# Products that nobody reads, in the pauses of TensorE at the end of attention and at the start of the experts

## The chip, the cores and the metric

The kernel runs on one core of one Trainium2 chip. The time is the device time of one execution in microseconds; of several executions the median is given. One more execution, under the hardware profiler, left the trace that the rows below come from.

## What is computed

Two stages follow each other. The first is cross attention with a causal mask, the second a routed feed-forward layer in which each token goes to one of 32 small experts.

```python
# x, ctx: (32, 256, 256) float32; 16 heads of 64; 32 experts with a hidden width of 64
q, k, v = layernorm(x) @ Wq, ctx @ Wk, ctx @ Wv            # 256 -> 1024, split into 16 heads
attn = softmax(where(causal_or_masked, -max, q @ k.T / 8))
x = x + (attn @ v) @ Wo + bo
n = layernorm(x).reshape(-1, 256)                          # 8192 tokens
e = argmax(n @ router_w.T + router_b)
x = x + relu(relu(n @ w1[e] + b1[e]) @ w2[e] + b2[e])
```

## The kernel before

**Attention phase.** Batches 0 to 31 run one after the other, and each batch in four quads of four heads (`QUADS`, index `s`). TensorE's work of a quad is written by hand in `iteration(b, prev, nxt)` (L675 ff.): the scores of the next quad in two halves, `scores(*ahead, 0, ...)` and `scores(*ahead, 1, ...)` (L584), between them the transposes of the normalised probabilities of this quad, `probs_t` (L629), then `values` of the quad before (L650, probabilities by V), then the `pieces`: projections for the next batch (L514), Wo of the batch before (L546), the transposes of its second layernorm (`x2`, L505) and its router logits (`lg`, L556). In the last batch there is no next batch, so most pieces are missing: in quad 2 only the transposes and the logits of batch 30 are left, in quad 3 none. `first_ready` and `second_ready` hold the waits ahead of `probs_t`: the probabilities must have been normalised by VectorE (L1109, L1112), which waits in turn for ScalarE's exponentials (L799).

`ranks` (L568) counts the tokens of a batch for each expert. VectorE turns these counts into row numbers (L992 to L1052), and GpSimd scatters the rows of the batch into the experts' lists in memory (L463, two scatters a batch).

**Behind the last batch** TensorE runs, in this order: ranks of batch 30, Wo of batch 31 in three parts with the last `values` between them, `busy(12)`, the transposes of batch 31 (they wait for its layernorm), `busy(2)`, its logits, `busy(6)`, ranks of batch 31 (they wait for the one-hot rows, L982), `busy(12)`. `busy(n)` issues n products of 512 columns (L673) whose results nobody reads.

**Expert phase.** The lists are cut in tiles of 128 tokens, taken in 48 pairs, u = 0, 1, 2 and so on in groups of `U` = 16. SyncE loads a pair's rows (`XS`, L1340). VectorE normalises them (`XH`, L1363) and at the end adds the residual (`Y`, L1373). TensorE does `turn` (4 transposes, L1473), `hid` (8 records, L1486) and `y_of` (4 records, L1496). ScalarE copies the transposes out (L1429) and applies relu (`HT`, L1436). GpSimd scatters the two tiles of the pair to the output (L1329). TensorE issues turn of pair u+4, hid of pair u+2 and y of pair u together; the first pairs are written out by hand (L1503 ff.), behind six unread products of 512 columns (L1503). In `hid` an unread product of 256 columns (L1483) stands ahead of each pair from u = 8 on.

A float32 product that isn't a transpose leaves two matmul records in the trace, so the six products of L1503 are 12 records; the products of `busy` leave one each.

Of the kernel before, what the change touches and what calls it, by code (L numbers as in the profile page):

```python
# [29 lines left out]
def attention_moe(nc, x, ctx, mask, Wq, Wk, Wv, Wo, bo, router_w, router_b, w1, b1, w2, b2, out):  # L30
# [21 lines left out]
    with ExitStack() as es:  # L52
# [240 lines left out]
        def G(b, s):  # L293

            return QUADS * b + s + 1
# [205 lines left out]
        def _(pe):  # L501
# [72 lines left out]
                last = transposes(dst, xn)  # L574
                last.then_inc(s_xt_pe, 1)

            def scores(b, s, i, between=None):
                p = 2 * s + i
                for it, o in ((0, 0), (1, P)):
                    if it and between:  # L580
                        between()
                    for side in range(2):
                        rows = slice(DH * side, DH * side + DH)
                        last = nc.tensor.matmul(psS[:, 2 * i + side, o:o + (it + 1) * P], QT[rows, p, it * P:(it + 1) * P],  # L584
                                                KT[rows, p, 0:(it + 1) * P], start=True, stop=True)
                last.then_inc(s_sc, 1)
# [17 lines left out]
            def first_ready(b, s, prev, nxt):  # L604

                pe.wait_ge(s_pn, 4 * G(b, s) - 2)
                if s > 0 or prev:
                    pe.wait_ge(s_pt, 3 * G(b, s) - 3)
                for bank, (name, at) in last_in(b, s, prev, nxt).items():
                    if bank < 2:  # L610
                        pe.wait_ge(*emptied(name, at))
# [57 lines left out]

            def busy(count):  # L670

                for _ in range(count):
                    nc.tensor.matmul(psS[:, 2, :], Wh["q"][:, 0, 0:P], Wh["q"][:, 0, 0:512], start=True, stop=True)  # L673

            def iteration(b, prev, nxt):  # L675
                for s in range(QUADS):
                    ahead = later(b, s + 1, nxt)
                    if ahead:
                        if s == 0 and prev and not (isinstance(b, int) and b == 1):

                            pe.wait_ge(s_pf, b - 1)
                        scores_may_start(*ahead)
                        scores(*ahead, 0, lambda: first_ready(b, s, prev, nxt))
                        probs_t(b, s, 0)
                        scores(*ahead, 1, lambda: second_ready(b, s, prev, nxt))
                        probs_t(b, s, 1)
                    else:
                        first_ready(b, s, prev, nxt)
                        probs_t(b, s, 0)
                        second_ready(b, s, prev, nxt)  # L690
                        probs_t(b, s, 1)
                    if s > 0:
                        values(b, s - 1, not prev and s == 1)
                    elif prev:
                        values(b - 1, QUADS - 1)
                    now = pieces(s, prev, nxt)
                    for n, (name, off) in enumerate(now):
                        if n < 3:
                            pe.wait_ge(s_pt, 3 * G(b, s) - 2 + n)
                        else:  # L700
                            pe.wait_ge(*emptied(now[n - 3][0], b + now[n - 3][1]))
                        piece(name, b + off, psR[:, banks(len(now))[n], :])
                        if s == QUADS - 1 and prev and n == 0:
                            ranks(b - 1, 8 * G(*ahead))
# [32 lines left out]
            values(B - 1, QUADS - 1)  # L737
            wo(B - 1, psR[:, 0, :], range(4, 6))
            wo(B - 1, psR[:, 0, :], range(6, PAIRS))
            busy(12)  # L740
            pe.wait_ge(s_xn2, 2 * B)
            transposes(psR[:, 1, :], xn2).then_inc(s_x2t_pe, 1)
            busy(2)
# [575 lines left out]
        with nc.Block(no_gpsimd_drain=True) as block2:  # L1319
# [140 lines left out]
            def _(pe):  # L1460
# [15 lines left out]
                def hid(i, u, free=True):  # L1476
                    pe.wait_ge(s_xht, U * i + u + 1)
                    for t in range(2):
                        pe.wait_ge(s_w1[t], U * i + u + 1)
                    if free:  # L1480
                        pe.wait_ge(s_h, U * i + u - 3)
                    if not isinstance(i, int) or i > 0 or u >= 8:
                        nc.tensor.matmul(psH[u % 2][:, 2 * P:4 * P], ident[:], W1R[:, 0:2, 0:P], start=True, stop=True)  # L1483
                    for c in range(KD):
                        for t in range(2):
                            last = nc.tensor.matmul(psH[u % 2][half(t), slot(u)], W1[u % W][:, t, c * HID:(c + 1) * HID], XHT[u % W][:, t, c, :],  # L1486
                                                    start=(c == 0), stop=(c == KD - 1))
                    last.then_inc(s_h_pe, 1)
# [10 lines left out]
                    last.then_inc(s_y_pe, 1)  # L1499

                pe.wait_ge(s_w1r, 16)
                for _ in range(6):
                    nc.tensor.matmul(psH[0][:, :], ident[:], W1R[:, 0:4, 0:P], start=True, stop=True)  # L1503
                pe.wait_ge(s_w2r, 32)
                pe.wait_ge(s_ht1, 1)
                turn(0, 0, False)
                turn(0, 1, False)
                hid(0, 0, False)
                turn(0, 2)
                for u in range(2):  # L1510
                    y_of(0, u, False)
# [45 lines left out]
```

## Time and profile before

| | us |
|---|---|
| median of 3 executions without the profiler | 1508.87 |
| lowest and highest of them | 1504.34, 1510.36 |
| the profiled execution, device time | 1513.0 |
| its span in the trace | 1511.3 |
| attention phase, to the last ranks | 0 to 1359.7 |
| expert phase, from the first turn | 1371.7 to 1511.3 |

The profiled execution lies above all three others. Sums are made in the trace, whose span lies 1.7 us below its device time. Granted clock 1.00 is TensorE at its full 2.4 GHz, 0.50 is 1.2 GHz. A row of the timeline gives the start of a group of like instructions, the time from its first start to its last end, and in square brackets how long the engine sat idle ahead of it and what ended that.

### The profile page before, as it was taken

How to read it: one execution, taken by the hardware profiler on the slowest of the kernel's cores; microseconds unless marked ns; L12 is line 12 of the kernel's file. 1: busy time of each engine (PE TensorE's matmuls, PEld its weight loads, DVE VectorE, ACT ScalarE, POOL GpSimd, SP SyncE). 2: the span in 40 equal slices, each digit the busy share in tenths (PEclk: the TensorE clock that was granted, in tenths of full speed). 3: DMA queues.
4: the chain of work that ended last, by engine and by line, in shares of the span. 5: the costliest groups of instructions: out<-in, count | busy, mean ns of one | idle time of the engine just before them, and what ended most of it. 6: DMA issues, size and time to landing. Idle time of an engine off the chain costs nothing.

```text
span 1511.3 us, 43956 instructions
## 1 busy us (share of the span) xinstructions
PE 1479.1 (98%) x14165; PEld 1283.4 (85%) x14165; DVE 1231.7 (82%) x5088; ACT 1013.6 (67%) x3144; POOL 360.6 (24%) x507
## 2 busy tenths in 40 slices
PE   8999999999999999999999999999999999978997
PEld 7898888888888888888888888888888888865775
DVE  5888888988888888888988888888888988755663
ACT  5767667667677667677666677677677677633663
POOL 3112212211121122222211121122222211112777
PEclk9999999999999999999999999999999999987998
DMA  8643000000000000000000000010000000005650
GB/s 288 128 150 115 29 21 29 29 22 29 29 22 25 25 29 29 27 23 29 29 22 29 28 23 22 29 29 29 23 27 29 29 22 22 15 8 175 212 174 12
DMA packets 70410, 77.85 MB, mean 52 GB/s; under 512 B 11351, under 2 KB 64221, under 8 KB 70369
## 3 DMA queue, kind: packets, MB, share of 16 engines
q1 hardware_dynamic: 62546, 60.37, 13.8%
q0 software_dynamic: 7680, 16.93, 3.1%
q8 instruction: 22, 0.36, 0.1%
q14 instruction: 18, 0.15, 0.0%
q10 hardware_dynamic: 144, 0.03, 0.0%
HBM read 47.61 MB, written 33.88 MB: 54 GB/s over the span
## 4 chain that ended last, share of the span: by engine, by line
PE 93%; DVE 3%; ACT 1%; DMA 1%; POOL 1%; issue 1%; SPq 0%; POOLq 0%; DVEq 0%
PE psR L514 37%; PE psS L584 14%; PE psO L650 12%; PE psR L546 12%; PE psR L629 6%; PE psS L1496 4%; PE psR L505 2%; PE psR L1486 2%; PE psR L556 2%; PE psR L1483 1%; PE psR L1473 1%; PE psO L1473 1%; DVE Sm L1112 0%; ACT Sm L799 0%; DMA lists<-stg,lrow 0%
## 5 line engine op out<-in xcount | busy, mean ns | idle before, releaser
L799 ACT ACTIVATE Sm<-Sm,mneg 128x128 f32<-128x128 f32 (+1 forms) x1024 | 453.5, 456 | 153.6 <-DVE mneg L1097 153.6
L1097 DVE CUSTOM_DVE_ANT_0 Sm<-psS,MK 128x128 f32<-128x128 f32 (+1 forms) x1024 | 303.7, 353 | 4.4 <-PE psS L584 1.9
L792 ACT ACTIVATE PT<-psR 128x512 f32<-128x512 f32 x384 | 201.6, 598 | 134.8 <-PE psR L629 130.9
L584 PE MATMUL psS<-KT,QT 64*128 64x128 f32 (+1 forms) x2048 | 251.5, 356 | 5.0 <-DVE V L774 2.0
L799 ACT ACTIVATION_READ_ACCUMULATOR Sm<-Sm,mneg 128x1 f32 x1024 | 205.5, 201 | 0.0
L650 PE MATMUL psO<-PT,V 128*64 128x256 f32 (+1 forms) x2048 | 196.0, 334 | 0.6 <-DVE OT_lo L1117 0.3
L1112 DVE SCALAR_TENSOR_TENSOR Sm<-Sm,halve,rinv 128x512 f32<-128x512 f32 x256 | 191.4, 748 | 0.0
L584 PEld LDWEIGHTS psS<-KT,QT 64*128 64x128 f32 x2048 | 148.7, 187 | 30.4 <-issue 7.7
L650 PEld LDWEIGHTS psO<-PT,V 128*64 128x64 f32 x2048 | 127.4, 137 | 49.0 <-DVE OT_lo L1117 1.2
L629 PEld LDWEIGHTS psR<-ident,Sm 64*128 64x128 f32 x3072 | 144.5, 139 | 21.1 <-DVE Sm L1112 2.5
L1103 DVE RECIPROCAL rinv<-rsum 128x4 f32<-128x4 f32 x256 | 44.1, 172 | 135.6 <-ACT Sm L799 132.3
L629 PE MATMUL psR<-ident,Sm 64*128 64x64 f32 x3072 | 140.9, 223 | 2.2 <-DVE Sm L1112 2.2
L1109 DVE SCALAR_TENSOR_TENSOR Sm<-Sm,halve,rinv 128x256 f32<-128x256 f32 x256 | 124.1, 485 | 9.1
L756 ACT ACTIVATE KT<-psR 128x512 f32<-128x512 f32 x128 | 75.6, 591 | 55.0 <-PE psR L514 55.0
L514 PE MATMUL psR<-CT_hi,Wk_hi 128*128 128x256 f32 x512 | 108.0, 293 | 1.3 <-ACT PT L792 1.3
L1329 POOL DMA_INDIRECT out<-Y,tok x96 | 94.0, 979 | 49.4 <-issue 27.4
L514 PE MATMUL psR<-XT_hi,Wq_hi 128*128 128x256 f32 x512 | 103.5, 284 | 2.0 <-DVE XT_lo L777 1.3
L514 PE MATMUL psR<-XT_lo,Wq_hi 128*128 128x256 f32 x512 | 103.3, 283 | 0.0
L756 ACT ACTIVATE QT<-psR 128x512 f32<-128x512 f32 x128 | 76.5, 598 | 39.8 <-PE psR L514 39.7
L514 PE MATMUL psR<-CT_lo,Wk_hi 128*128 128x256 f32 x512 | 103.0, 283 | 0.0
L514 PE MATMUL psR<-XT_hi,Wq_lo 128*128 128x256 f32 x512 | 103.0, 283 | 0.0
L514 PE MATMUL psR<-CT_hi,Wk_lo 128*128 128x256 f32 x512 | 102.7, 282 | 0.0
(155 smaller groups left out, 3061.7 us busy)
## 6 DMA issues: line engine op xcount, KB each, us to landing
lists<-pad SPq DMA_DIRECT2D x8, 1560.0 KB, 10.2
XS<-lists SPq DMA_DIRECT2D x48, 260.0 KB, 2.9
x_in<-in_x SPq DMA_DIRECT2D x32, 256.0 KB, 3.0
ctx_in<-in_ctx SPq DMA_DIRECT2D x32, 256.0 KB, 2.6
xr<-in_x SPq DMA_DIRECT2D x32, 256.0 KB, 2.6
W2R<-in_L_ffn_weights SPq DMA_DIRECT2D x1, 2048.0 KB
out<-Y,tok POOLq DMA_INDIRECT x96, 2.4
W2R<-in_L_xattn_Wv SPq DMA_DIRECT2D x2, 512.0 KB, 9.3
```

What stands on the lines that cost most here:

```text
L514: last = nc.tensor.matmul(dst, a(k), z(k), start=(n == 0), stop=(n == 3 * len(ks) - 1))
L546: last = nc.tensor.matmul(dst[:, it * D:(it + 1) * D], a[:, t, rows], z[:, t, :], start=(it == 0 and a is OTh and z is Woh and t == 0), st ...
L584: last = nc.tensor.matmul(psS[:, 2 * i + side, o:o + (it + 1) * P], QT[rows, p, it * P:(it + 1) * P], KT[rows, p, 0:(it + 1) * P], start=T ...
L629: last = nc.tensor.transpose(ring[:, o:o + DH], Sm[rows, 2 * (s % 2) + i, side, src:src + P], ident[rows, rows])
L650: last = nc.tensor.matmul(psO[DH * side:DH * side + DH, i * N + t * P:(i + 1) * N], V[:, t, DH * h:DH * h + DH], blocks_of[:, blocks, :, : ...
L756: nc.scalar.activation(T[:, 2 * c:2 * c + 2, :].rearrange("p a n -> p (a n)"), src[:, :], ACT.Copy).then_inc(done, 1)
L792: nc.scalar.activation(PT[:, s % 2, 512 * k:512 * k + 512], psR[:, k, :], ACT.Copy).then_inc(s_pt, 1)
L799: nc.scalar.activation(v, v, ACT.Exp, bias=mneg[:, s % 2, k:k + 1], scale=-1.0, accum_out=rsum[:, s % 2, k:k + 1]).then_inc(s_exp, 1)
L1097: nc.vector.tensor_tensor_reduce(out=Sm[:, 2 * (s % 2) + i, side, cols], in0=psS[:, 2 * i + side, cols], in1=MK[:, cols], scale=-SCALE, sc ...
L1109: nc.vector.scalar_tensor_tensor(out=v, in0=v, scalar=halve[:, 0:1], in1=of[:, :, 0:1].broadcast_to([P, 2, P]), op0=ALU.mult, op1=ALU.mult ...
L1112: nc.vector.scalar_tensor_tensor(out=v, in0=v, scalar=halve[:, 1:2], in1=of[:, :, 1:2].broadcast_to([P, 2, N]), op0=ALU.mult, op1=ALU.mult ...
L1329: nc.gpsimd.indirect_dma_start(out_rows, bass.IndirectOffsetOnAxis(ap=tok[u][:, t:t + 1], axis=0), Y[u][:, t, :], None, bounds_check=last_ ...
```

## The change

Five places on TensorE get more products that nobody reads. No other instruction is added, taken away or moved.

- In the last batch, quad 2: three products of 128 columns (64 rows deep) between the parts of the first half of the scores, ahead of the wait for normalised probabilities, and two in the second half.
- In the last batch, quad 3: `busy(5)` ahead of the first wait and `busy(4)` ahead of the second. `busy` itself now waits first until the last scores have been read, since it writes into their bank.
- Behind the last Wo: `busy(20)` where `busy(12)` stood.
- In `hid` the product of 256 columns stands ahead of each pair from u = 1 on, not from u = 8: seven more.
- At the start of the expert phase: seven products of 512 columns where six stood, and two of 128 columns each behind the turn of pair 0 and the hid of pair 0 (`still(2)`).

```diff
-            def scores(b, s, i, between=None):
+            def scores(b, s, i, between=None, still=0):
                 p = 2 * s + i
                 for it, o in ((0, 0), (1, P)):
                     if it and between:
+                        for _ in range(still):
+                            nc.tensor.matmul(psS[:, 2 * i, 3 * P:4 * P], ident[0:DH, :], ident[0:DH, :], start=True, stop=True)
                         between()
...
             def busy(count):
 
+                pe.wait_ge(s_sm, 8 * G(B - 1, QUADS - 1))
                 for _ in range(count):
                     nc.tensor.matmul(psS[:, 2, :], Wh["q"][:, 0, 0:P], Wh["q"][:, 0, 0:512], start=True, stop=True)
...
-                        scores(*ahead, 0, lambda: first_ready(b, s, prev, nxt))
+                        scores(*ahead, 0, lambda: first_ready(b, s, prev, nxt), 3 if s == 2 and not nxt else 0)
                         probs_t(b, s, 0)
-                        scores(*ahead, 1, lambda: second_ready(b, s, prev, nxt))
+                        scores(*ahead, 1, lambda: second_ready(b, s, prev, nxt), 2 if s == 2 and not nxt else 0)
                         probs_t(b, s, 1)
                     else:
+                        busy(5)
                         first_ready(b, s, prev, nxt)
                         probs_t(b, s, 0)
+                        busy(4)
                         second_ready(b, s, prev, nxt)
...
-            busy(12)
+            busy(20)
             pe.wait_ge(s_xn2, 2 * B)
...
-                    if not isinstance(i, int) or i > 0 or u >= 8:
+                    if not isinstance(i, int) or i > 0 or u >= 1:
                         nc.tensor.matmul(psH[u % 2][:, 2 * P:4 * P], ident[:], W1R[:, 0:2, 0:P], start=True, stop=True)
...
-                for _ in range(6):
+                for _ in range(7):
                     nc.tensor.matmul(psH[0][:, :], ident[:], W1R[:, 0:4, 0:P], start=True, stop=True)
                 pe.wait_ge(s_w2r, 32)
                 pe.wait_ge(s_ht1, 1)
+                def still(count):
+                    for _ in range(count):
+                        nc.tensor.matmul(psY[3][:, 0:P], ident[:], W1R[:, 0, 0:P], start=True, stop=True)
+
                 turn(0, 0, False)
+                still(2)
                 turn(0, 1, False)
                 hid(0, 0, False)
+                still(2)
                 turn(0, 2)
```

TensorE in the last batch, quads 2 and 3, before. `Sm` are the probabilities, `xn2` and `X2T` the second layernorm of batch 30 and its transpose:

```order
L584 MATMUL psS<-KT,QT 128x128 x2
L584 MATMUL psS<-KT,QT 128x256 x2
L629 MATMUL psR<-ident,Sm 128x64 x8
L584 MATMUL psS<-KT,QT 128x128 x2
L584 MATMUL psS<-KT,QT 128x256 x2
L629 MATMUL psR<-ident,Sm 128x64 x16
```

The same place after, on through quad 3 (the four rows of `values`, L652, left out):

```order
L586 MATMUL psS<-KT,QT 128x128 x2
L582 MATMUL psS<-ident 128x128 x3
L586 MATMUL psS<-KT,QT 128x256 x2
L631 MATMUL psR<-ident,Sm 128x64 x8
L586 MATMUL psS<-KT,QT 128x128 x2
L582 MATMUL psS<-ident 128x128 x2
L586 MATMUL psS<-KT,QT 128x256 x2
L631 MATMUL psR<-ident,Sm 128x64 x16
...
L505 MATMUL psR<-ident,xn2 128x128 x4
L556 MATMUL psR<-rwT,X2T 128x32 x4
L676 MATMUL psS<-Wq_hi 128x512 x5
L631 MATMUL psR<-ident,Sm 128x64 x8
L676 MATMUL psS<-Wq_hi 128x512 x4
L631 MATMUL psR<-ident,Sm 128x64 x16
```

The new rows stand ahead of the four waits for `Sm`, and nothing else has moved.

TensorE at the start of the expert phase, before; the number behind a name is the pair's:

```order
L1503 MATMUL psR<-W1R,ident 128x512 x6
L1473 MATMUL psO<-ident,XH0 128x128 x4
L1473 MATMUL psR<-ident,XH1 128x128 x4
L1486 MATMUL psR<-XHT0,W1_0 64x128 x4
L1473 MATMUL psO<-ident,XH2 128x128 x4
```

and after, as far as the hid of pair 1:

```order
L1508 MATMUL psR<-W1R,ident 128x512 x7
L1478 MATMUL psO<-ident,XH0 128x128 x4
L1513 MATMUL psS<-W1R,ident 128x128 x2
L1478 MATMUL psR<-ident,XH1 128x128 x4
L1491 MATMUL psR<-XHT0,W1_0 64x128 x4
L1513 MATMUL psS<-W1R,ident 128x128 x2
L1478 MATMUL psO<-ident,XH2 128x128 x4
...
L1488 MATMUL psR<-W1R,ident 128x256
L1491 MATMUL psR<-XHT1,W1_1 64x128 x4
```

Each hid from pair 1 on now has an L1488 ahead of it, and the turns of pairs 1 and 2 each have two small products ahead.

## Rows read from the trace of the kernel before

**Rows 1.** The page's second part, granted clock in 40 slices.
```profile
PEclk9999999999999999999999999999999999987998
```

**Rows 2.** Windows: length, busy of PE, PEld, DVE, ACT, POOL, clock, DMA share, GB/s.
```profile
1331.00:1341.00 10.00, 6.61 (x61) 4.82 (x60) 4.83 (x22) 6.30 (x20) 0.00 (x0) 0.66 0.01 2
1352.00:1362.00 10.00, 8.39 (x33) 6.50 (x34) 4.16 (x26) 0.60 (x1) 0.72 (x1) 0.66 0.00 1
1370.00:1375.00 5.00, 2.67 (x19) 1.55 (x17) 3.19 (x12) 1.39 (x3) 0.00 (x0) 0.96 1.01 308
1390.00:1395.00 5.00, 5.00 (x34) 4.03 (x33) 3.10 (x12) 4.00 (x10) 2.25 (x3) 0.83 0.33 106
```

**Rows 3.** Timeline of TensorE, last batch: start us, us, engine, line.
```profile
1325.92 0.70 PE L584 MATMUL psS<-KT,QT 64*128 64x256 f32 x4 [0.92 <-DVE Sm L1112]
1327.79 0.70 PE L584 MATMUL psS<-KT,QT 64*128 64x256 f32 x4 [0.65 <-DVE Sm L1112]
1332.30 1.05 PE L556 MATMUL psR<-rwT,X2T 128*128 128x32 f32 x8 [0.90 <-ACT X2T L766]
1334.47 0.69 PE L629 MATMUL psR<-ident,Sm 64*128 64x64 f32 x8 [1.12 <-DVE Sm L1112]
1336.25 1.12 PE L629 MATMUL psR<-ident,Sm 64*128 64x64 f32 x16 [1.09 <-DVE Sm L1112]
1337.64 2.83 PE L650 MATMUL psO<-PT,V 128*64 128x256 f32 x16 [0.28 <-DVE OT_lo L1117]
1343.58 1.52 PE L650 MATMUL psO<-PT,V 128*64 128x256 f32 x16
```

**Rows 4.** Timeline of all engines, behind the last Wo to the expert phase.
```profile
1348.07 2.91 PE L673 MATMUL psS<-Wq_hi 128*128 128x512 f32 x12
1349.91 0.69 DVE L943 TENSOR_TENSOR stg<-psR,xr 128x512 f32<-128x512 f32 x1 [3.44 <-DMA lists<-stg,lrow]
1353.61 0.67 PE L505 MATMUL psR<-ident,xn 128*128 128x128 f32 x4 [2.63 <-DVE xn L959]
1354.96 1.92 PE L556 MATMUL psR<-rwT,X2T 128*128 128x32 f32 x8
1356.69 2.91 PE L673 MATMUL psS<-Wq_hi 128*128 128x512 f32 x6
1358.23 0.22 DVE L982 TENSOR_TENSOR OH<-iota_e,eid 128x64 bf16<-128x64 f32 x1
1359.40 0.28 PE L568 MATMUL psS<-OH,upto 128*128 128x32 bf16 x2
1365.10 5.42 PE L1503 MATMUL psR<-W1R,ident 128*128 128x512 f32 x12 [0.62 <-DVE tile_row L1358]
```

**Rows 5.** Timeline, start of the expert phase, and the last scatter.
```profile
1371.69 0.72 PE L1473 MATMUL psO<-ident,XH 128*128 128x128 f32 x4 [1.18 <-DVE XH L1363]
1373.56 0.74 PE L1473 MATMUL psR<-ident,XH 128*128 128x128 f32 x4 [1.15 <-DVE XH L1363]
1376.08 2.07 PE L1496 MATMUL psS<-W2R,HT 65*128 x4
1391.96 1.13 PE L1496 MATMUL psS<-W2R,HT 65*128 x4
...
1394.63 0.97 POOL L1329 DMA_INDIRECT out<-Y,tok  x1 [2.45 <-DVE Y L1373]
...
1508.62 0.97 POOL L1329 DMA_INDIRECT out<-Y,tok  x1 [0.30 <-issue]
```

**Rows 6.** Timeline of TensorE, one pair with its unread product, full clock.
```profile
1397.15 0.63 PE L1473 MATMUL psO<-ident,XH 128*128 128x128 f32 x4
1397.62 0.60 PE L1483 MATMUL psR<-W1R,ident 128*128 128x256 f32 x2
1398.73 1.13 PE L1496 MATMUL psS<-W2R,HT 65*128 x4
1399.70 0.51 PE L1473 MATMUL psR<-ident,XH 128*128 128x128 f32 x3
```

## The prediction

> **What bounds the kernel now.** I read the page's slices of granted clock first. They are full but for the first slices and for two near the end [rows 1]. A change of unread products can give time only where the clock is low, so the question is what stands in those stretches. Windows over the end show three, in each of which the clock fell to 0.50, that is 1.2 GHz, and came back to 2.4 GHz. A mean of 0.66 over 10 us is 6.8 us at 0.50: once between 1331 and 1341, once between 1352 and 1362. The third is long: a mean of 0.96 up to 1375 puts its start at 1374.6, one of 0.83 from 1390 on puts its end at 1391.7 [rows 2]. Then I read the timeline for what TensorE did ahead of each fall. Ahead of the first it waited for ScalarE and VectorE: pauses of 0.92 and 0.65, then 0.90 between a few small products and 1.12 [rows 3]. Ahead of the second it sat 2.63 us [rows 4]. Ahead of the third there were pauses of 1.18 and 1.15 [rows 5]. So the falls follow pauses that add up, and the change puts products into just these.
>
> Behind these stretches another engine holds the end. From the scatter at 1394.63 to the one at 1508.62 GpSimd issues 90 scatters, 113.99/89 = 1.28 us each, with no idle time but their own 0.30 of issue between them [rows 5]. A pair has two, 2.56 us; TensorE needs 1399.70 - 1397.15 = 2.55 us for a pair [rows 6]. The end is thus "start of the unbroken row of scatters + 90 x 1.28". The time is saved only by what makes that row start earlier.
>
> **Part 1, last batch.** Quad 2 gets 3 + 2 products of 128 columns, each two records. By the nearest row, 4 transposes of 128 columns in 0.47 us (from its start to that of the next line) [rows 6], a record is 0.12: 0.7 us in a pause of 0.92 and 0.47 in one of 0.65 [rows 3]. They fit. `busy(5)` starts behind the logits, at about 1333.2; one product of it is 0.24 us at full clock (12 in 2.91 us [rows 4]), so it ends at 1334.4, ahead of the transposes at 1334.47. `busy(4)`, 0.96, fits in the 1.09 ahead of 1336.25 with 0.1 to spare. The new wait inside `busy` is for scores that VectorE finished reading at about 1331; nothing queues behind it. What the clock gives: `values` of quad 2 took 2.83 us at half speed, the same work at full speed 1.52 [rows 3]. Its start, 1337.64, stays, since it waits for VectorE's OT_lo: the 0.4 us that the transposes ahead gain are not on the path. **Gain 1.3 us**; bounds 0 (the clock falls all the same) and 1.3. It carries on: ranks of batch 30 feed VectorE, the list scatter, and L943, which waits 3.44 us for that scatter's landing and not for Wo [rows 4]. Wo itself moves up by the same 1.3, so neither takes the place of the other.
>
> **Part 2, behind the last Wo.** `busy(20)` lasts 20 x 0.24 = 4.8 where 2.9 stood, in a gap of 2.9 + 2.63: about 0.75 us of pause stay (by starts, 0.22 a product, 1.2). If the clock stays up: the logits, at 1354.96 because they wait for ScalarE's copy, take 1.05 [rows 3] instead of 1.92 [rows 4], and end at 1356.0. The one-hot rows came 1358.45 - 1356.88 = 1.57 behind the logits' end, so 1357.6. `busy(6)`, 6 x 0.24 = 1.45, is through by 1357.3 and covers itself. At half clock it took 2.91 and held the ranks until 1359.40, 0.95 behind the one-hot rows [rows 4]. Ranks now at 1357.65: **gain 1.75 us**, bounds 0 and 1.75. What is next late there is VectorE's chain to the row numbers, unchanged.
>
> Behind these ranks `busy(12)` is now over at full speed, 2.9 us after them, and the products of L1503 start 5.7 us after them (1365.10 - 1359.40 [rows 4]). The pause of 2.8 us, with one small transpose in it, is as long as the 2.63 that preceded a fall. So in part of the executions the clock will fall here. I price that at nothing: the 14 records of L1503 take 14 x 0.45 = 6.3, the pause to the first turn was 1.18 and takes the seventh product's 0.9; a low stretch as long as the first two, 6.8 us [rows 2], would cost 3.4 if it lay on these products alone; they run without a pause, which the others did not, so I take half, 1.7, which pushes the first turn by about 1.4, and the next turn waits for its rows at 1373.56 anyway [rows 5]. Bounds 0 and 2 us lost.
>
> **Part 3, expert phase.** In the clock of before, if TensorE stays at 2.4 GHz: steps are turn 0.47, unread product and hid 1.11, y 2.55 - 1.58 = 0.97 [rows 6]. y of pair 0 starts at 1376.0 as before, since it waits for ScalarE's HT; hid of pair 0, still(2) and turn 2 (0.6 + 0.47 + 0.47 from 1374.25) end at 1375.8 and lie beside that wait. y of pair 0 took 2.07 [rows 5] and takes 0.97, to 1377.0. Then hid 1 and turn 3, 1.58; y of pair 1 waits 0.4 more for its HT and runs 1379.0 to 1380.0; hid 2, turn 4, hid 3, turn 5 take 3.16, y of pair 2 runs 1383.15 to 1384.1; hid 4, turns 6 and 7, hid 5 take 3.16, y of pair 3 starts at 1387.3. Before it started at 1391.96 and its scatter followed at 1394.63, 2.67 later [rows 5]. Now its scatter is due at 1389.95. GpSimd is free by then (pair 2's two scatters end at 1388.3). From there TensorE makes a pair in 2.55 and GpSimd takes 2.56, so the row stays unbroken: **gain 4.7 us**. The unread products of pairs 1 to 5 are in this sum; those of pairs 6 and 7 hide behind GpSimd. Bounds: 4.7 up, and below zero down, which is a rival.
>
> A rule to weigh: the clock came back at 1391.7 [rows 2], just ahead of y of pair 3 at 1391.96 [rows 5], so behind the hids and turns that stand between y of pair 2 and that one, and half of these are transposes. The Trainium skill, "TensorE: Matmul & The Clock Gate", Part 4, says that in a transpose the full clock isn't engaged, since it doesn't count as busy work in the same way. By that rule the opening, rich in transposes, would stay at half speed as before, and the result would be the first rival's. The trace speaks against it.
>
> **Sum.** 1.3 + 1.75 + 4.7 = 7.75, less nothing. 1513.0 - 7.8 = 1505.2 for an execution like the profiled one. The median of before is 1508.87, so against it 3.7 us, 0.25%. The runs of before spread from 1504.34 to 1510.36; by my reading the low one is an execution in which the long low stretch was missing or short, and it checks the sum: without part 3's stretch the profiled one would be at about 1508, without any at 1505. The change should above all make the slow executions like the fast one.
>
> **Rivals.** (a) The clock falls in the opening all the same. For: after the change pauses of about 0.6 us are left ahead of turns 0 and 1, with a pause's worth of waiting on HT. Against: they are half as long as before and products stand between. Then the unread products cost up to 2 x 0.53 = 1.06 each at half clock, and five of them stand ahead of pair 3: with the same 17 us low, 1513.0 - 3.05 + 5.3 = 1515.3; with a stretch as short as the first two, about 1509. Chance 0.12. (b) The same, but the clock doesn't come back. In the half state a pair takes about 2 x 2.55 = 5.1 us against GpSimd's 2.56, so each pair beyond the fourth breaks the row of scatters and adds 2.5 us: one more pair gives 1517.8, two 1520.4. It decides as soon as the low stretch outlasts that of before. This ends slower by over 0.5% (above 1516.4). Chance 0.05. (c) The products miss: one of the first two stretches stays and the opening gains, or the other way round, or the executions of before were mostly without the long stretch; nothing is to be seen, 1507.5 to 1509.5. Chance 0.09. (d) `busy(4)` or `busy(5)` outlasts its cover because the clock has fallen before it: 0.24 more for each, 2.2 us in all, less the 1.3 of `values`; about 1 us lost, in the range, no case of its own. (e) More than forecast, below 1501.3: it would need 3.8 us that no row offers, since the main loop is untouched; 0.03.
>
> **Chances.** Forecast 0.71, rivals as given. A measurement of this kernel tells about 0.5%, 7.5 us, from no change. Faster by more 0.03; within 0.91; slower by more 0.06. The range goes from 1503.0 (a little under the fastest run of before) to 1509.5, which takes in (c) and the short form of (a).
>
> **What would show it.** In the trace after: granted clock 1.00 through 1330 to 1345 and 1350 to 1358, `values` of quad 2 at 1.5 us, ranks of batch 31 about 3.05 us earlier; no idle time of the first products beyond 0.3 us; clock 1.00 from the first turn on, y of pair 3 some 7.7 us earlier, and GpSimd's row unbroken from its fourth pair. A low stretch of about 3 us around L1503 would not matter. I am wrong if the opening still shows 0.50 over many us, if TensorE and not GpSimd ends last at the scatters, or if the transposes at 1334.47 and 1336.25 have become late.

## The result, and the profile after

| us | before | changed |
|---|---|---|
| median of 16 executions each | 1509.61 | 1504.66 |
| lowest and highest | 1504.34, 1514.36 | 1501.86, 1506.27 |
| profiled execution: device time, span | 1513.0, 1511.3 | 1501.86, 1500.1 |

The ratio is 0.9968, with a 95% interval from 0.9954 to 0.9982: 4.9 us faster by the medians, clear of noise, and within the 0.5% that had been set as "no change". 1505.2 had been forecast. The spread narrows from 10 us to 4.4.

The ratios in this text are those on record. They aren't the quotients of the medians, and where a kernel's executions fall into groups the two can differ.

The profiled execution of the changed kernel is its fastest, that of before lies near its slow end, and so their spans differ by 11.2 us, more than twice what the medians do. The clock of the two pages says why. The second part of the page after, which answers [rows 1]:

```profile
PEclk9999999999999999999999999999999999999999
```

The windows after, columns as in [rows 2]: the two of 10 us that had 0.66, the edge before the long low stretch and the 15 us inside it:

```profile
1331.00:1341.00 10.00, 9.17 (x94) 7.03 (x93) 7.66 (x40) 3.58 (x10) 0.03 (x1) 1.00 0.01 2
1352.00:1362.00 10.00, 7.51 (x30) 4.18 (x29) 6.96 (x39) 0.31 (x1) 2.04 (x2) 1.00 0.08 27
1370.00:1375.00 5.00, 4.65 (x35) 3.31 (x36) 3.38 (x12) 2.42 (x7) 2.54 (x3) 1.00 1.09 359
1375.00:1390.00 15.00, 15.00 (x110) 11.49 (x112) 9.09 (x32) 10.88 (x27) 9.15 (x10) 1.00 0.64 206
```

All three low stretches are gone. So is a fourth, which has nothing to do with the change: in the first batch, where TensorE's instructions are the same in both kernels. Windows from 24 to 34 us, first of before, then of after:

```profile
24.00:34.00 10.00, 7.38 (x50) 6.11 (x51) 6.01 (x24) 3.04 (x8) 0.50 (x2) 0.66 0.98 302
```

```profile
24.00:34.00 10.00, 7.07 (x69) 6.45 (x70) 5.86 (x25) 4.47 (x14) 0.49 (x2) 1.00 0.97 305
```

0.66 over 10 us is 6.8 us at 1.2 GHz in before, none in after. It is worth 3 us: the first scores of the last batch's quad 2 stand at 1324.51 in one trace and at 1321.53 in the other, ahead of anything the change touches. These 3 us of the 11.2 aren't the change's: of the eleven traces of this case without added products in the first batch, five show full clock there, five have 6.8 us at half clock and one 3.4.

The rest by place. The timeline after; the L652 row answers that of L650 at 1337.64 in [rows 3], the next five answer [rows 4], the last four [rows 5] (L1478 turn, L1501 y):

```profile
1330.22 1.41 PE L676 MATMUL psS<-Wq_hi 128*128 128x512 f32 x5
1331.56 0.47 PE L631 MATMUL psR<-ident,Sm 64*128 64x64 f32 x8
1334.68 1.52 PE L652 MATMUL psO<-PT,V 128*64 128x256 f32 x16 [0.69 <-DVE OT_lo L1122]
...
1348.70 0.66 PE L505 MATMUL psR<-ident,xn 128*128 128x128 f32 x4 [0.19 <-DVE xn L964]
1350.05 1.08 PE L556 MATMUL psR<-rwT,X2T 128*128 128x32 f32 x8 [0.22 <-ACT X2T L771]
1350.96 1.62 PE L676 MATMUL psS<-Wq_hi 128*128 128x512 f32 x6
1352.84 0.20 PE L568 MATMUL psS<-OH,upto 128*128 128x32 bf16 x2 [0.26 <-DVE OH L987]
1358.45 6.28 PE L1508 MATMUL psR<-W1R,ident 128*128 128x512 f32 x14 [0.62 <-DVE tile_row L1363]
...
1364.90 0.71 PE L1478 MATMUL psO<-ident,XH 128*128 128x128 f32 x4 [0.18 <-DVE XH L1368]
1368.55 1.12 PE L1501 MATMUL psS<-W2R,HT 65*128 x4
...
1380.24 1.13 PE L1501 MATMUL psS<-W2R,HT 65*128 x4
```

GpSimd's first scatter of pair 3 and the last one, answering those of [rows 5], and one between them:

```profile
1382.92 0.97 POOL L1334 DMA_INDIRECT out<-Y,tok  x1 [1.86 <-DVE Y L1378]
...
1438.53 0.98 POOL L1334 DMA_INDIRECT out<-Y,tok  x1 [0.95 <-DVE Y L1378]
...
1497.48 0.97 POOL L1334 DMA_INDIRECT out<-Y,tok  x1 [0.30 <-issue]
```

| from | to | before | after | gained | forecast |
|---|---|---|---|---|---|
| start | values of quad 2 | 1337.64 | 1334.68 | 2.96 | 0 |
| values of quad 2 | ranks of batch 30 | 2.76 | 1.46 | 1.30 | 1.3 |
| these ranks | transposes of batch 31 | 13.21 | 12.56 | 0.65 | 0 |
| the transposes | ranks of batch 31 | 5.79 | 4.14 | 1.65 | 1.75 |
| these ranks | first turn | 12.29 | 12.06 | 0.23 | 0 |
| first turn | y of pair 3 | 20.27 | 15.34 | 4.93 | 4.7 |
| y of pair 3 | its scatter | 2.67 | 2.68 | 0 | 0 |
| its scatter | last scatter | 113.99 | 114.56 | -0.57 | 0 |

In these two traces each of the three gains is within 0.25 us of its forecast. Where nothing had been forecast, 0.65 and 0.23 were gained and 0.57 lost. The 0.65 is the landing of the second list scatter: from its start to that of VectorE's L943 (L948 after), which waits for it, the traces have 3.29 us before (1346.62 to 1349.91) and 2.65 after (1342.35 to 1345.00). The change doesn't touch either.

The experiments show that these terms aren't yet the reason for the difference of the medians.

### The profile page after: what moved, and what is told of

It reads as the page before. It is cut to its first block, busy times and chain, and to the rows that moved or that the text cites. A ratio compares the mean times of both kernels' runs of the same rounds, so it can differ in the third digit from the quotient of the medians.

```text
span 1500.1 us, 44058 instructions
## 1 busy us (share of the span) xinstructions
PE 1473.2 (98%) x14216; PEld 1280.3 (85%) x14216; DVE 1230.8 (82%) x5088; ACT 1012.3 (67%) x3144; POOL 360.3 (24%) x507
## 4 chain that ended last, share of the span: by engine, by line
PE 93%; DVE 3%; ACT 1%; POOL 1%; DMA 1%; issue 1%; SPq 0%; ACTq 0%; POOLq 0%; DVEq 0%
PE psR L514 37%; PE psS L586 14%; PE psO L652 12%; PE psR L546 12%; PE psR L631 6%; PE psS L1501 3%; PE psR L505 2%; PE psR L1491 2%; PE psR L556 2%; PE psR L1488 1%; PE psR L1478 1%; PE psO L1478 1%; POOL out L1334 0%; DVE Sm L1117 0%; ACT Sm L804 0%
## 5 line engine op out<-in xcount | busy, mean ns | idle before, releaser
L652 PE MATMUL psO<-PT,V 128*64 128x256 f32 (+1 forms) x2048 | 194.7, 332 | 1.1 <-DVE OT_lo L1122 0.7
L652 PEld LDWEIGHTS psO<-PT,V 128*64 128x64 f32 x2048 | 126.7, 136 | 49.1 <-DVE OT_lo L1122 4.5
L631 PEld LDWEIGHTS psR<-ident,Sm 64*128 64x128 f32 x3072 | 143.3, 138 | 19.4 <-DVE Sm L1117 0.9
L631 PE MATMUL psR<-ident,Sm 64*128 64x64 f32 x3072 | 139.7, 221 | 0.1
L392 POOL CAST first_masked<-maskrow 128x1 f32<-128x1 uint8 x32 | 5.9, 183 | 406.6 <-DMA maskrow<-in_mask_BxS_bf 406.6
```

The source lines that it names most:

```text
L631: last = nc.tensor.transpose(ring[:, o:o + DH], Sm[rows, 2 * (s % 2) + i, side, src:src + P], ident[rows, rows])
L652: last = nc.tensor.matmul(psO[DH * side:DH * side + DH, i * N + t * P:(i + 1) * N], V[:, t, DH * h:DH * h + DH], blocks_of[:, blocks, :, : ...
```

## The experiments

Three rounds of four kernels. The first round came to a chip that takes 1548.0 us for the kernel before; the other two to one like the first (1509.2 and 1509.8). Ratios are to the kernel before of the same round.

**The products of attention alone.** Edits against the changed kernel:

```diff
-                    if not isinstance(i, int) or i > 0 or u >= 1:
+                    if not isinstance(i, int) or i > 0 or u >= 8:
...
-                for _ in range(7):
+                for _ in range(6):
...
-                still(2)      # both places
```

> Only the products of the last batch and the 20 behind the last Wo; the expert phase is that of the kernel before. My theory: ranks of batch 31 come 3 us earlier against the first scores of the last batch than in the trace of before, values of quad 2 takes 1.5 us, and the whole gains 3 us: a median near 1506.5 where the changed kernel has 1504.7. The opening of the expert phase still falls to half clock in part of the executions, so they stay spread by 6 us or more. Rival, the gain of this part is lost again in the expert phase: median at the kernel before, within 1 us.

> Only the products of the last batch and the 20 behind the last Wo, again, for a chip of the first kind. Theory as before: 3 us under the kernel before in every execution, so a median near 1506, but still spread over 6 us or more, since the opening falls to half clock in part of the executions. Rival: within 1 us of the kernel before.

On the slow chip 1542.52 against 1548.0, ratio 0.9963 (0.9949 to 0.9977). On the usual one 1501.92 against 1509.75, ratio 0.9949 (0.9931 to 0.9967), six executions from 1500.74 to 1505.73. I had expected 3 us and got 7.8, and the spread came out at 5.0 where 6 or more had been expected. By the medians this half of the change is faster alone than the whole (1501.92 against 1504.66 and 1506.07). That isn't clear of noise: the intervals of the ratios overlap, and the two never ran in the same round.

**The products of the expert phase alone.** The other half: no products in quads 2 and 3, `busy(12)` behind the last Wo.

> Only the products of the expert phase; the last batch and what stands behind its last Wo are as before. My theory: the low stretches at the last batch and behind the last Wo come back and cost 3 us, the opening stays at full clock in every execution: median near 1507.5, spread under 5 us, values of quad 2 at 2.8 us, y of pair 3 about 15.5 us after the first turn as in the changed kernel. Rival, the whole gain is the opening's: median 1504.7, like the changed kernel.

> Only the products of the expert phase, again, for a chip of the first kind. Theory: the slow executions of the kernel before go (none above 1510), its fast ones stay where they are, and the median is near 1507.5, 3 us above the changed kernel. Rival: the changed kernel's median.

Slow chip: 1543.83, ratio 0.9970 (0.9959 to 0.9981). Usual one: 1509.65, ratio 0.9995 (0.9983 to 1.0008), twelve executions from 1507.60 to 1511.62. The executions above 1512 went (the kernel before has five of 16 in this round from 1512.4 to 1514.6), but so did those below 1507.6 (it has three, from 1505.88). The median doesn't move. That the low end would stay where it is was wrong, and so was that none would lie above 1510: six of the twelve do.

Its windows over the two low stretches of attention, and over the opening:

```profile
1331.00:1341.00 10.00, 6.74 (x66) 5.29 (x67) 5.64 (x25) 5.28 (x18) 0.00 (x0) 0.83 0.00 0
1350.00:1360.00 10.00, 7.12 (x27) 5.61 (x28) 3.54 (x21) 0.60 (x1) 0.94 (x2) 0.66 0.00 1
1370.00:1390.00 20.00, 18.64 (x132) 13.58 (x131) 12.16 (x42) 11.68 (x28) 6.19 (x7) 1.00 0.86 279
```

The first two are back, the third stays away. Against it the attention half, from its first turn on:

```profile
1368.00:1388.00 20.00, 18.71 (x141) 13.96 (x140) 14.39 (x48) 14.81 (x36) 9.14 (x10) 1.00 0.90 285
```

It too is at full clock in the opening, without any product added there. So in this pair of traces, both at full clock, one can read what the opening's products cost. From the first turn to y of pair 3 it takes (turn and y of the attention half, then of the opening half, whose y is L1499):

```profile
1367.72 0.63 PE L1478 MATMUL psO<-ident,XH 128*128 128x128 f32 x4
...
1381.31 1.13 PE L1501 MATMUL psS<-W2R,HT 65*128 x4
```

```profile
1371.44 0.72 PE L1476 MATMUL psO<-ident,XH 128*128 128x128 f32 x4 [0.35 <-DVE XH L1366]
...
1387.31 1.13 PE L1499 MATMUL psS<-W2R,HT 65*128 x4
```

13.59 us without the products, 15.87 with them, 20.27 in the trace of before with the long low stretch. Against a trace whose clock falls there they save 4.4 us; against one whose clock doesn't they cost 2.3. The row of scatters adds to the cost: from the scatter of pair 3 to the last it takes 114.64 us in the opening half and 113.88 in the attention half.

**The changed kernel without the seven products ahead of the hids of pairs 1 to 7** (the line `u >= 8` again, the rest stays).

> The changed kernel without the seven products of 256 columns ahead of the hids of pairs 1 to 7; the small ones and the seven of 512 columns stay. Theory: five of them stand on the path to y of pair 3, 0.53 us each, and the turns and hids keep the clock up without them. Then y of pair 3 comes 2.6 us earlier (12.8 us after the first turn), the unbroken row of scatters starts as much earlier, and the median is about 1502.5. Rival, it is these products that hold the clock: the granted clock falls to 0.5 in the opening and the median is 1508 or more, with single executions above 1512.

> The changed kernel without the seven products ahead of the hids of pairs 1 to 7, again, for a chip of the first kind. With these products the pair of runs at a cold start differed by 2.1 us (1506.53 and 1504.42). Theory: 2 us under the changed kernel, 1503 to 1504, and no low stretch of over 7 us in the opening. Rival: more executions with a long low stretch, median 1505 or more.

Slow chip: 1541.47, 0.9957 (0.9942 to 0.9972). Usual one: 1502.24, 0.9951 (0.9934 to 0.9967), six executions from 1499.57 to 1504.43; first turn to y of pair 3 13.75 us (1364.90 to 1378.65), no low stretch in the opening. 2.4 us under the changed kernel's 1504.66 by the medians, if of another round. The first theory had 2.6 us, all from y of pair 3. The traces give 15.34 - 13.75 = 1.6 there, and 0.7 more from the row of scatters, 113.86 us instead of 114.56.

On the slow chip this kernel's trace shows what the rival had named, a clock that falls in the opening:

```profile
1379.11 0.72 PE L1478 MATMUL psR<-ident,XH 128*128 128x128 f32 x4 [1.90 <-ACT XHT L1434]
```

```profile
1375.00:1385.00 10.00, 8.10 (x47) 5.89 (x47) 4.84 (x17) 6.42 (x16) 4.09 (x5) 0.78 0.57 189
1385.00:1395.00 10.00, 10.00 (x39) 7.04 (x39) 3.19 (x11) 3.64 (x10) 4.86 (x5) 0.50 0.45 150
```

It fell behind a pause of 1.90 us and stayed low for 17.1 us. The attention half's trace on that chip fell at the same place, behind 1.78. The two traces there with the products ahead of the hids, the opening half and the kernel of the next experiment, have 1.00 from 1375 to 1390 and no pause over 0.35 us. On the usual chip the kernel without them held the clock. So these products may well hold it where the opening is disturbed. Whether that pays on the slow chip stays open, since the changed kernel itself never ran there.

**Products for the first batch**, added to the changed kernel:

```diff
-  lambda: first_ready(b, s, prev, nxt), 3 if s == 2 and not nxt else 0)
+  lambda: first_ready(b, s, prev, nxt), 3 if s == 2 and not nxt else 7 if s == 0 and not prev else 0)
...
-  lambda: second_ready(b, s, prev, nxt), 2 if s == 2 and not nxt else 0)
+  lambda: second_ready(b, s, prev, nxt), 2 if s == 2 and not nxt else 2 if s == 0 and not prev else 0)
```

> The changed kernel with seven and two more unread products of 128 columns in the first batch, in the pauses of 1.8 and 0.65 us ahead of its first transposes. Theory: the trace of before has a low stretch of 6.8 us at 26 to 33 us that the one of after doesn't have, though no instruction differs there; it comes in part of the executions of both and costs 3 us. With the products it goes: median about 1502.5, spread 2 us instead of 4.4. Rival, the spread of the changed kernel comes from elsewhere (memory, the main loop): median 1504.7 and the same spread.

It ran on the slow chip alone: 1539.11, ratio 0.9935 (0.9919 to 0.9952), the best of that round. The spread that its expectation speaks of was not to be seen there (1535.39 to 1540.07), and its trace has full clock in the first batch. So have the other two traces with these products, against five of eleven without.

**The changed kernel again, and both edits together.**

> The changed kernel itself, beside the others of this call on the same chip. The chip of the first four experiments took 1548 us for the kernel before where the first chip took 1509.6: its attention phase was as long, the expert phase some 35 us longer. If this chip is like the first, 1504.7; if like the second, the ratio of 0.9968 says 1543, and the parts measured there (0.9963 and 0.9970, together 0.9933) say 1537.6.

> The changed kernel with the nine small products of the first batch, and without the seven of 256 columns ahead of the hids of pairs 1 to 7. Theory: both gains add, 2 us from the first batch and 2.6 us from the opening: 4.6 us under the changed kernel of the same call on a chip like the first. On one like the second, where the scatters are not an unbroken row, an earlier start of the row is partly given back: 2 to 4 us. Rival: the opening falls to half clock without its products more often than with them and eats the gain: within 1 us of the changed kernel.

The changed kernel: 1506.07, ratio 0.9965 (0.9949 to 0.9981). Its twelve executions fall into two groups, four from 1503.06 to 1503.63 and eight from 1505.90 to 1506.87, with nothing between; the mean granted clock over the span is 0.996 in each of the first and 0.993 to 0.994 in the second. The upper group is the larger one, so the quotient of the medians is 0.998; the means, 1505.37 and 1510.21, give 0.9968. Both edits: **1501.67**, ratio 0.9944 (0.9923 to 0.9964), seven executions from 1500.85 to 1501.85. It is 4.4 us under the changed kernel, 7.5 under the kernel before, 4.6 had been expected against the changed one, and its spread is 1 us. Its timeline in the first batch:

```profile
23.43 0.49 PE L586 MATMUL psS<-KT,QT 64*128 64x128 f32 x4
23.75 1.72 PE L582 MATMUL psS<-ident 64*128 64x128 f32 x14
25.66 0.70 PE L586 MATMUL psS<-KT,QT 64*128 64x256 f32 x4 [0.18 <-DVE V L781]
26.17 0.44 PE L631 MATMUL psR<-ident,Sm 64*128 64x64 f32 x8
26.41 0.47 PE L586 MATMUL psS<-KT,QT 64*128 64x128 f32 x4
26.68 0.61 PE L582 MATMUL psS<-ident 64*128 64x128 f32 x4
27.53 0.70 PE L586 MATMUL psS<-KT,QT 64*128 64x256 f32 x4 [0.24 <-DVE V L781]
```

The wait for V, 1.78 us of idle time before, holds 14 records now and 0.18 of idle time. With both edits the upper of the two groups is gone. That it was the first batch alone isn't shown: no trace of an upper execution was taken, and this kernel differs in the opening too. The profiled execution of the changed kernel in this round, one of the lower group, has half of the stretch in the first batch:

```profile
24.00:34.00 10.00, 7.61 (x61) 6.73 (x62) 6.02 (x24) 3.54 (x10) 0.50 (x2) 0.83 0.97 305
```

The means of the groups, 0.002 to 0.003 apart, stand for 6 to 9 us more at 1.2 GHz, more than the other 3.4 us of the first batch. So another place probably takes part. The last batch can be it, for there the clock still falls in some executions, in spite of the products. The fastest kernel's own trace, the one just shown, does it:

```profile
1331.00:1341.00 10.00, 10.00 (x85) 7.65 (x86) 7.31 (x35) 4.00 (x12) 0.00 (x0) 0.83 0.01 2
```

```profile
1330.87 2.02 PE L676 MATMUL psS<-Wq_hi 128*128 128x512 f32 x5
1332.81 0.69 PE L631 MATMUL psR<-ident,Sm 64*128 64x64 f32 x8
1333.43 1.82 PE L676 MATMUL psS<-Wq_hi 128*128 128x512 f32 x4
1335.83 1.52 PE L652 MATMUL psO<-PT,V 128*64 128x256 f32 x16
```

0.83 is 3.4 us at 1.2 GHz. `busy(5)` and `busy(4)` took 2.02 and 1.82 us instead of 1.41 and 1.19, the transposes stood behind them, and `values` started 5.85 us behind the logits instead of 5.34. Both traces of the cold start below show the same, 0.5 us each.

The products of the first batch seem to have a small price. In the three traces with them the first scores of the last batch's quad 2 start at 1322.20 to 1322.76, in the five that had full clock without them at 1321.33 to 1322.58, and in the five with 6.8 us at half clock at 1323.93 to 1325.09. Of the 3 us some 2 are left, which is what had been expected.

**A cold start of the expert phase**, one product of 512 columns ahead of the first turn instead of seven (`range(1)`), once with the products ahead of the hids and once without.

> The changed kernel with one product of 512 columns ahead of the first turn instead of seven, so that TensorE stands still for some 5 us there and the first turn meets the half clock. This is the case of the forecast's rivals a and b. Theory: the clock comes back within 10 us, since unread products stand among the pairs' own; y of pair 3 about 17 to 18 us after the first turn instead of 15.3; 1 to 2 us slower than the changed kernel. Rival b: it stays at half clock for 15 us or more and the kernel is 5 us or more slower.

> As the one before it, but also without the seven products ahead of the hids of pairs 1 to 7. If these bring the clock back sooner than the pairs' own work does, this is slower than the one before it, by 3 us or more (a low stretch of 17 us as in the trace of before). If they only cost their time, it is 2 to 5 us faster (five of them on the path to y of pair 3, at 0.53 to 1.06 us).

With them 1506.53, ratio 0.9980 (0.9964 to 0.9996), 0.5 us over the changed kernel of that round; without them 1504.42, ratio 0.9954 (0.9939 to 0.9969). Timeline of the first, then of the second:

```profile
1369.13 1.10 PE L1478 MATMUL psO<-ident,XH 128*128 128x128 f32 x4 [5.53 <-DVE XH L1368]
...
1385.24 1.13 PE L1501 MATMUL psS<-W2R,HT 65*128 x4
```

```profile
1368.59 1.10 PE L1478 MATMUL psO<-ident,XH 128*128 128x128 f32 x4 [5.42 <-DVE XH L1368]
...
1383.20 1.13 PE L1501 MATMUL psS<-W2R,HT 65*128 x4
```

The first turn takes 1.10 and not 0.72, since the clock is at 1.2 GHz behind 5.5 us of idle time. It came back inside 1368 to 1378 in both: the windows there have a mean of 0.80 with the products and 0.82 without. So rival b, a clock that doesn't come back, didn't happen in this trace though the fall was forced, and the products didn't bring it back sooner than the pairs' own work did: 6.8 us low in both. With the pairs' own work alone it has also stayed low for 17.1 us (before, and the slow chip's trace shown above), so 6.8 isn't what it always takes. They cost 16.11 - 14.61 = 1.5 us on the way to y of pair 3.

**No unread product in the whole expert phase behind `still`**, added to the fastest kernel:

```diff
-                    if not isinstance(i, int) or i > 0 or u >= 8:
-                        nc.tensor.matmul(psH[u % 2][:, 2 * P:4 * P], ident[:], W1R[:, 0:2, 0:P], start=True, stop=True)
```

> The fastest kernel so far (nine small products in the first batch, none ahead of the hids of pairs 1 to 7; 1501.67) with no unread product ahead of any hid. TensorE then needs 2.1 us for a pair instead of 2.55. Theory: the end is the first unbroken scatter plus 90 times 1.28 us on GpSimd, so TensorE's 0.44 us in each of 40 pairs, 17 us in all, gain nothing: 1501 to 1502. Rival one: TensorE is a bound beside GpSimd, 2 us or more faster. Rival two: without them the clock falls in the middle of the phase and stays low, since a pair then takes over 4 us: 1510 or more.

1502.75, ratio 0.9950 (0.9935 to 0.9966), six executions from 1502.31 to 1503.29: 1 us more than with them, in another round. Windows of the phase:

```profile
1388.00:1470.00 82.00, 82.00 (x620) 66.37 (x619) 60.82 (x184) 62.03 (x153) 62.62 (x64) 1.00 0.59 175
1470.00:1490.00 20.00, 1.15 (x6) 0.67 (x4) 1.69 (x5) 0.00 (x0) 15.31 (x16) 0.58 0.05 12
```

TensorE is done shortly after 1470 and stands still, VectorE and ScalarE with it, and GpSimd goes on scattering to 1498.26, its 89 steps at 1.29 us. From the scatter at 1383.14 to that one it is 115.12 us, where the fastest kernel had 114.01 and the changed one 114.56. 0.44 us taken from each of 40 pairs on TensorE gained nothing. The end is GpSimd's; why its steps are 0.01 us longer here stays open. The clock stayed at 1.00 up to 1470 with the pairs' own work alone.

**The slow chip.** Its attention phase is as long as elsewhere: in the kernel without the seven products the first turn stood at 1364.87 there and at 1364.90 on the usual chip. Its expert phase isn't. The waits of 1400 to 1480 there (engine, line, waited for; total, times, longest), and the windows of the same stretch there and in the changed kernel:

```profile
POOL out L1334 <- DVE Y L1378: 22.8, 12, 2.8
ACT HT L1441 <- remote: 21.1, 8, 4.6
DVE Y L1378 <- remote: 19.2, 5, 5.6
```

```profile
1400.00:1480.00 80.00, 72.78 (x427) 52.53 (x424) 36.48 (x120) 37.89 (x95) 47.05 (x48) 0.85 0.50 152
```

```profile
1400.00:1480.00 80.00, 80.00 (x568) 61.19 (x568) 49.67 (x156) 51.02 (x126) 60.44 (x63) 1.00 0.49 150
```

ScalarE and VectorE stand for up to 5.6 us at a time on something outside the trace's engines ("remote"), GpSimd issues 48 scatters where it issues 63, and the clock falls again and again, to a mean of 0.85. What they wait for stays open.

**Where the clock fell, trace by trace.** Windows of 2 us over every trace give the time at 1.2 GHz ahead of TensorE's last work (behind it each trace has 6 us or more, which cost nothing). "Products" are the unread ones added at the place of the row.

| place | traces without products | traces with products |
|---|---|---|
| first batch | 11: five none, one 3.4 us, five 6.8 us | 3: none |
| last batch | 3: all 6.8 us | 11: eight none, three 3.4 us |
| behind the last Wo | 3: all 6.8 us | 11: nine none, two 3.4 us, both behind the ranks of batch 31 |
| opening (ahead of the hids), usual chip | 5: four none, one 17.1 us (before) | 3: none |
| opening, slow chip | 2: 17.1 and 23.9 us | 2: none |

The opening's rows go by the products ahead of the hids, as far as 1400, and leave out the two cold starts. These are counts of single executions; on the usual chip they are too few to say how often the opening falls with or without products.

## Why the prediction was right

**The number.** 1513.0 - 7.8 = 1505.2, measured 1504.66. The sum was made for an execution like the profiled one of before, which had the low stretch of the first batch. Eight of the 16 executions of the changed kernel in the first measurement lie at 1505.24 to 1506.27 with a mean clock of 0.993 to 0.994, the other eight at 1501.86 to 1504.08 with 0.995 to 0.998. If the first are those with that stretch, which no trace shows, the sum is right within 1.1 us like for like, and the median lies lower because half of the executions don't have it. The prediction didn't see this stretch at all: its windows cover the end only, and it called the first slices of [rows 1] less than full, where all of them are 9.

**Part 1** stands as forecast: 1.30 of 1.3. The 0.69 of idle time ahead of `values` shows that the earlier transposes were not on the path. `busy(5)` ended ahead of the probabilities, and so did `busy(4)`: no idle time and no delay of note ahead of L631, the first at 1331.56, the shift of 2.91 against 1334.47 being that of everything else. In this trace rival d didn't occur. It did in three of the eleven traces with these products: the clock fell under `busy(5)` all the same, and 0.5 us of the 1.3 was lost, as shown above.

**Part 2**: 1.65 of 1.75, with the ranks now waiting 0.26 for the one-hot rows and no longer for `busy(6)`. `busy(20)` filled the gap to 0.19 us. The clock did fall behind these ranks in other executions, as thought possible: in the attention half alone there is a low stretch of about 3.4 us from 1361.4, and ranks to first turn took 12.56 us there against 12.06. That is 0.5 us of the 0 to 2 allowed.

**Part 3** is right for the pair of traces, 4.93 of 4.7 (y of pair 0 came 0.66 us sooner behind the first turn than the sum had it, and the steps to y of pair 3 took 0.4 more), and wrong as a statement on the change. The step that failed is the premise that a typical execution of before has the long low stretch. I took it from one trace, and the text itself noted that this trace was slower than all three other executions. Of 62 executions of before on the usual chips 24 lie from 1511.99 to 1515.00 and 38 from 1504.34 to 1511.32. In the two rounds that list each execution's clock (46 of them) nothing lies between 1511.23 and 1512.36, and the upper group has a mean of 0.984 to 0.986 and the lower of 0.988 to 0.993; 0.005 over a span of 1507 us is 15 us more at half clock, which fits the stretch of 17. That the stretch is what makes the upper group is inferred from this; no second trace of it was taken.

In an execution that keeps its clock in the opening the products there cost 2.3 us on the way to y of pair 3 and save nothing. The bounds of part 3 went "below zero" only through a clock that falls all the same; that the clock might not fall in the kernel before was missing among them, and it is the commoner case. The opening half alone, ratio 0.9995, fits the two cases averaged: an estimate from the traces has 24 of 62 executions gain 4.4 less 0.65 for the row of scatters, and 38 lose 2.3 and 0.75, together a loss of 0.4 us; the ratio has a gain of 0.8, with 1.2 lost and 2.6 gained as its bounds. So the attention half brings the gain of the medians.

The end of the sum, 1505.2, holds all the same, since it is the time of an execution without the three stretches, whatever before has. What it had wrong is what a typical execution of before loses, and so gains, in the opening. That the median came within 0.6 us of it is partly luck, for half of the executions seem to lack the stretch of the first batch, which the sum left in without knowing of it.

**The unbroken row** was broken a little: -0.57. Part 3 put TensorE at 2.55 and GpSimd at 2.56 us a pair, took them to be even, and let the unread products of pairs 6 and 7 "hide behind GpSimd". That term was put at nothing and isn't nothing. Without a product TensorE needs 2.11 us from y of pair 3 to y of pair 4 (1391.96 to 1394.07 before), with it 2.55 (1380.24 to 1382.79). So before, TensorE gets ahead of GpSimd in pairs 4 to 7, and after the change it doesn't. In each of the four traces on the usual chip with the products ahead of these hids one pair comes late some 55.6 us into the row, GpSimd sits idle 0.87 to 0.98 us ahead of it (here 0.95, at 1438.53), and the row takes 114.56 to 114.64 us. In the five traces there without them (before among them; the kernel with no product ahead of any hid, 115.12, left out) no pair is late, and it takes 113.86 to 114.01. Between the changed kernel and the one without the seven products nothing else differs, so the products are the cause; that it works through the lead of pairs 4 to 7 is read from the traces and no run isolates it.

**Rivals.** (a) and (b) weren't seen in any trace of a kernel with the opening's products; the forced cold start cost 0.5 us by the medians, where the forecast had thought of 4 to 15. There the sum in (a) counted 17 us low in the opening; it was about 7 us, and over before y of pair 0 began at 1373.56. (c) had the right premise about the kernel before, that most executions lack the long stretch, and the wrong time: it said 1507.5 to 1509.5 and "nothing is to be seen". The Trainium skill's rule on transposes ("TensorE: Matmul & The Clock Gate", Part 4) isn't borne out here as a rule for an opening rich in transposes: the attention half's trace has 1.00 from 1368 to 1388, where about a quarter of TensorE's time goes to turns (some 0.6 of 2.1 us a pair). What a stretch of transposes alone would do no run shows.

**What stays open.** The attention half alone had been given 3 us and got 7.8. 3.0 of these are its own two terms. The long low stretch of the opening, which none of the six executions seems to have, doesn't explain the rest: without the five executions above 1512 the kernel before still has a median of 1509.35 in that round, 7.4 us above this half. In the two traces, both with 6.8 us low in the first batch, the first turn comes 3.97 us earlier (1367.72 against 1371.69). Where the other 3 to 4 us of the medians come from isn't shown, and six executions are few.

Nor is it shown when the long stretch comes. The opening of this half has the same instructions as before's. Whether ending attention at full clock keeps the fall away, or six executions were too few, is open: at 40% each, six without it come about one time in twenty, and on the slow chip the trace of this half does fall, for 23.9 us from 1380 on.

## What to carry to other kernels

An unread product pays where the clock would fall, and costs its own duration, or part of it, where it wouldn't. So look at the clock of several executions before you put any on the critical path. In a pause of an engine it was free here as long as the clock held, and cost 0.5 us where the clock fell under it. A place between an engine's own products isn't free. When the engine that ends the program works in an unbroken row, count what starts that row earlier, and don't slow the engine that feeds it at the start of the row: the lead that it wins there seems to cover a late piece further on.

## What the runs showed of the hardware

The same instructions ran at full clock in one execution and had 6.8 us at half clock in another, in the first batch. In the opening, too, the same instructions had 17.1 us at half clock in one trace (before) and none in another (the attention half). In the first batch that makes 3 us, twice the gain of part 1, and a profile of one execution doesn't tell whether such a stretch is in every execution. Two chips of one kind differed by 38 us in this kernel, nearly all of it in the phase that scatters its output, while two traces of one kernel, one of each chip, reached the first turn within 0.03 us of each other (1364.87 and 1364.90).
